# First edge stage of a graph network: target terms from limbs kept in SBUF, two one-hots and two products per tile

## What is computed

```
h = (x @ W).reshape(-1, H, F)
el = (h * attn_l).sum(-1)
er = (h * attn_r).sum(-1)
e = leaky_relu(el[src] + er[dst], 0.2)
emax = segment_max(e, dst)
ee = exp(e - emax[dst])
alpha = ee / segment_sum(ee, dst)[dst]
rst = segment_sum(h[src] * alpha[:, :, None], dst)
```

## Time and profile before

| what | value |
|---|---|
| median of 3 runs | 12361.57 us (12352.24 to 12380.39) |
| profiled execution, its own time | 12351.98 us |
| its span in the trace | 12350.2 us |
| node stage of layer 0 writes its tables | 176 to 205 us |
| first edge stage | 205 to 3578 us |
| last edge stage | 9832 to 12284 us |
| transfers of limbs | 1632 of 3.0 KB |
| gathers of the first edge stage | 1612 |

### The profile page before, as it was taken

One profiled execution on the slowest core, in us unless ns is written; L12 is line 12 of the kernel. 1 busy time (PEld: TensorE's weight loads), 2 busy tenths in 40 slices (PEclk: granted clock), 3 DMA queues, 4 the chain that ended last, 5 costly groups with the idle time before them and its releaser, 6 DMA issues. The chain is left out here.

```text
span 12350.2 us, 151587 instructions
## 1 busy us (share of the span) xinstructions
PE 6147.4 (50%) x29478; PEld 5149.9 (42%) x29478; DVE 6427.4 (52%) x17554; ACT 1847.1 (15%) x3224; POOL 7271.6 (59%) x6460
## 2 busy tenths in 40 slices
PE   1332333333345555555554677777777644444443
PEld 1222222222234444455454566666666533333332
DVE  3444444444456777666666566666666533332234
ACT  0111111111112222211111111111111200000001
POOL 2445444544517888888887455555555466666664
PEclk7555555555555555555555788788777755555555
DMA  3322322223256677777777211111111111111111
GB/s 84 75 76 70 77 75 72 74 75 76 71 102 111 111 108 111 112 108 110 113 108 117 55 39 39 39 39 40 40 38 39 43 44 43 43 43 43 44 43 44
DMA packets 1090391, 862.21 MB, mean 70 GB/s; under 512 B 408696, under 2 KB 925183, under 8 KB 1089702
## 3 DMA queue, kind: packets, MB, share of 16 engines
q0 software_dynamic: 386880, 430.42, 20.5%
q1 hardware_dynamic: 702220, 427.58, 14.0%
q10 hardware_dynamic: 1036, 1.96, 0.1%
HBM read 709.41 MB, written 149.81 MB: 70 GB/s over the span
## 5 line engine op out<-in xcount | busy, mean ns | idle before, releaser
L1274 POOL DMA_INDIRECT sums<-sumrows,index x1612 | 2527.6, 1568 | 710.4 <-issue 311.3
L663 POOL DMA_INDIRECT rows<-table,index x1612 | 1614.1, 1001 | 1890.4 <-DMA index<-in_src_batches 1414.4
L1415 POOL DMA_INDIRECT rows<-table,index x1612 | 1587.7, 985 | 1298.1 <-DVE mid L1472 741.9
L1611 POOL DMA_INDIRECT rows<-table,index x1612 | 1530.6, 949 | 1010.5 <-issue 475.6
L1672 PE MATMUL psS<-hot,rows 128*128 128x128 f32 x3224 | 1024.0, 476 | 1445.0 <-issue 655.4
L1672 PEld LDWEIGHTS psS<-hot,rows 128*128 128x128 f32 x3224 | 793.5, 313 | 1675.4 <-issue 888.9
L801 DVE TENSOR_TENSOR ACC<-ACC,psA 128x128 f32 x1612 | 462.9, 287 | 1682.3 <-remote 836.3
L1242 PE MATMUL psX<-same,hotW 128*128 128x128 f32 x3224 | 811.2, 431 | 987.3 <-DVE hotW L1145 744.7
L1242 PEld LDWEIGHTS psX<-same,hotW 128*128 128x128 f32 x3224 | 702.8, 321 | 1109.1 <-DVE hotW L1145 849.4
L1644 DVE TENSOR_TENSOR ACC<-ACC,psS 128x128 f32 x1612 | 465.8, 289 | 1258.6 <-issue 686.6
L1506 PEld LDWEIGHTS psS<-hot,mid 128*128 128x128 f32 x6448 | 1092.6, 240 | 64.1 <-issue 3.0
(11 more groups left out here) (306 smaller groups left out, 9781.0 us busy)
## 6 DMA issues: line engine op xcount, KB each, us to landing
win<-table SPq DMA_DIRECT2D x1612, 64.5 KB
srow<-src_f SPq DMA_DIRECT2D x403, 256.0 KB
rows<-table,index POOLq DMA_INDIRECT x4836
HN<-rel_f SPq DMA_DIRECT2D x102, 512.0 KB, 4.4
relB<-rel_f SPq DMA_DIRECT2D x102, 512.0 KB, 6.1
er<-limbs SPq DMA_DIRECT2D x1632, 3.0 KB
sums<-sumrows,index POOLq DMA_INDIRECT x1612
ACC<-edge_marks SPq DMA_DIRECT2D x204, 96.0 KB
```

Of the source, the lines that this page charges most:

```text
L663: nc.gpsimd.indirect_dma_start(out=rows[:, r, k, :], out_offset=None, in_=table0[:, :], in_offset=bass.IndirectOffsetOnAxis(ap=index[:, r, ...
L1274: nc.gpsimd.indirect_dma_start(out=sums1[u][:, :], in_=sums[:, s, u, :], in_offset=None, compute_op=ALU.add, out_offset=bass.IndirectOffse ...
L1415: nc.gpsimd.indirect_dma_start(out=rows[:, n % R, u, :], out_offset=None, in_=table2[:, :], in_offset=bass.IndirectOffsetOnAxis(ap=index[: ...
L1611: nc.gpsimd.indirect_dma_start(out=rows[:, n % R, u, :], out_offset=None, in_=table3[:, :], in_offset=bass.IndirectOffsetOnAxis(ap=index[: ...
```

## The change

The limbs of all nodes stay in SBUF as `LIMB`, 128 nodes by 50 blocks (the last of zeros), and are not written to DRAM. A tile's destinations lie in the block of its first destination or the next one. Positions are relative to the start of that block, 0 to 255, so ScalarE makes two one-hots (own block and the next, `far`), and TensorE takes two products which accumulate. The block number is a register on PE, read from `B0F` by `blocks`. SP loads no limbs. Three of the four zero fills are issued behind the loads of batches 3, 4 and 5.

```diff
-        D0 = sb("D0", [1, T], I32)
+        first_rows = sb("first_rows", [2 * 32, T], I32)
+        D0, B0F = first_rows[0:1, :], first_rows[32:33, :]
+        LIMB = sb("LIMB", [P, TN + 1, 3, H], BF16)
...
+        def blocks(eng, tile):
+
+            _, firsts = nc.values_load_multi_w_load_instructions(
+                B0F[0:1, bass.ds(tile, U)], engines=(eng.engine,), min_val=0, max_val=N // P,
...
                             sp.wait_ge(s_limbs, 1)
-                            sp.dma_start(limbs[0:TN * P, :].rearrange("(t p) c -> p t c", p=P), LIMB[:, :, :, :].rearrange("p t l h -> p t (l h)")).then_inc(s_out, 16)
-                            sp.dma_start(limbs[TN * P:NPAD, :], LIMB[:, 0, :, :].rearrange("p l h -> p (l h)")).then_inc(s_out, 16)
-                        sp.wait_ge(s_out, 32 if limbs is None else 64)
+                        sp.wait_ge(s_out, 32)
...
-                        nc.vector.tensor_tensor(rel[:, :, :], edge[:, :, :], first, ALU.subtract).then_inc(s_rel, 1)
+                        link(nc.vector.tensor_scalar(block_i[:, :, :], edge_i[:, :, 0:1], ~(P - 1), None, ALU.bitwise_and))
+                        link(nc.vector.tensor_copy(block_v[:, :, :], block_i[:, :, :]))
+                        nc.vector.tensor_tensor(rel[:, :, :], edge[:, :, :], block_v[:, :, :].to_broadcast([TP, TT, P]), ALU.subtract).then_inc(s_rel, 1)
...
-                        dve.wait_ge(s_in, 16 * 5)
+                        dve.wait_ge(s_in, 16 * 6)
                         nc.vector.tensor_copy(src_v[:, :], src_i[:, :]).then_inc(s_float, 1)
+                        link(nc.vector.tensor_scalar(B0F[:, :], B0F[:, :], 7, None, ALU.logical_shift_right))
...
-            hotT = sb("hotT0", [P, 2, PIECE, P], BF16)
+            hotT = sb("hotT0", [P, 2, 2, PIECE, P], BF16)
...
                         for q in range(pieces):
-                            for k in range(q * PIECE, (q + 1) * PIECE):
-                                if k % U == 0:
-                                    firsts = windows(sp, n * B0 + k)
-                                sp.dma_start(er[:, r, k, :], limbs0[bass.ds(firsts[k % U], P), :]).then_inc(s_erw[r], 16)
-                        for q in range(pieces):
-                            wait_over(sp, s_hotT, (n - 1) * pieces + (q + 1))
+                            wait_over(sp, s_abs, (n - 1) * pieces + (q + 1))
...
+                    for r in range(R):
+                        load(R + r, 1, r)
+                        zeros(r)
+                    with sp.Fori(2, BATCHES // R) as g:
                         for r in range(R):
                             load(R * g + r, g, r)
-                    for k in range(COPIES):
-                        sp.dma_start(sums1[k].rearrange("(t p) c -> p t c", p=P), K[:, CZ:CEND].unsqueeze(1).to_broadcast([P, NPAD // P, W1])).then_inc(s_clear, 16)
+                    zeros(R)
...
-                            nc.scalar.activation(relB[q], relB[q], ACT.Abs, bias=K[:, CN:CN + 1]).then_inc(s_abs, 1)
+                            own, far = (hotT[:, q % 2, b, :, :].rearrange("p t e -> p (t e)") for b in range(2))
+                            nc.scalar.activation(far, relB[q], ACT.Abs, bias=K[:, CF:CF + 1]).then_inc(s_far, 1)
+                            nc.scalar.activation(own, relB[q], ACT.Abs, bias=K[:, CN:CN + 1]).then_inc(s_abs, 1)
+                            act.wait_ge(s_far, n * pieces + (q + 1))
+                            nc.scalar.activation(far, far, ACT.Relu, bias=K[:, C1:C1 + 1], scale=-1.0)
                             act.wait_ge(s_abs, n * pieces + (q + 1))
-                            nc.scalar.activation(own, relB[q], ACT.Relu, bias=K[:, C1:C1 + 1], scale=-1.0).then_inc(s_hotT, 1)
+                            nc.scalar.activation(own, own, ACT.Relu, bias=K[:, C1:C1 + 1], scale=-1.0).then_inc(s_hotT, 1)
...
-                        pe.wait_ge(s_erw[r], 16 * B0 * g + 16 * B0)
...
-                                done = nc.tensor.matmul(psE[:, k * 3 * H:(k + 1) * 3 * H], hotT[:, q % 2, k % PIECE, :], er[:, r, k, :], start=True, stop=True)
+                                if k % U == 0:
+                                    starts = blocks(pe, n * B0 + k)
+                                own = psE[:, k * 3 * H:(k + 1) * 3 * H]
+                                nodes2 = LIMB[:, bass.ds(starts[k % U], 2), :, :]
+                                nc.tensor.matmul(own, hotT[:, q % 2, 0, k % PIECE, :], nodes2[:, 0, :, :].rearrange("p l h -> p (l h)"), start=True, stop=False)
+                                done = nc.tensor.matmul(own, hotT[:, q % 2, 1, k % PIECE, :], nodes2[:, 1, :, :].rearrange("p l h -> p (l h)"), start=False, stop=True)
```

More of the change, by code:

```diff
@@ L51, in constants @@
     k[:, C1] = 1.0
+    k[:, CF] = -(P + np.arange(P))
     k[0:3, CO:CZ] = 1.0
@@ L190, in windows @@
                 D0[0:1, bass.ds(tile, U)], engines=(eng.engine,), min_val=0, max_val=N,
+                skip_runtime_bounds_check_because="a dst is a node number, and padding edges end at N")
+            return firsts
+        def blocks(eng, tile):
+            _, firsts = nc.values_load_multi_w_load_instructions(
+                B0F[0:1, bass.ds(tile, U)], engines=(eng.engine,), min_val=0, max_val=N // P,
                 skip_runtime_bounds_check_because="a dst is a node number, and padding edges end at N")
@@ L280, in _ @@
                             value = TAB[:, :, width - H:width]
-                            link(nc.vector.tensor_copy(LIMB[:, :, 0, :], value))
-                            link(nc.vector.tensor_tensor(rest[:, :, :], value, LIMB[:, :, 0, :], ALU.subtract))
-                            link(nc.vector.tensor_copy(LIMB[:, :, 1, :], rest[:, :, :]))
-                            link(nc.vector.tensor_tensor(rest[:, :, :], rest[:, :, :], LIMB[:, :, 1, :], ALU.subtract))
-                            nc.vector.tensor_copy(LIMB[:, :, 2, :], rest[:, :, :]).then_inc(s_limbs, 1)
+                            nc.vector.memset(limbs[:, TN:TN + 1, :, :], 0.0)
+                            link(nc.vector.tensor_copy(limbs[:, 0:TN, 0, :], value))
+                            link(nc.vector.tensor_tensor(rest[:, :, :], value, limbs[:, 0:TN, 0, :], ALU.subtract))
+                            link(nc.vector.tensor_copy(limbs[:, 0:TN, 1, :], rest[:, :, :]))
+                            link(nc.vector.tensor_tensor(rest[:, :, :], rest[:, :, :], limbs[:, 0:TN, 1, :], ALU.subtract))
+                            nc.vector.tensor_copy(limbs[:, 0:TN, 2, :], rest[:, :, :]).then_inc(s_limbs, 1)
                     @block.scalar
@@ L476, in build @@
                 edge = sb("edge", [TP, TT, P])
+                block_i = sb("block_i", [TP, TT, 1], I32)
+                block_v = sb("block_v", [TP, TT, 1])
                 ends_i = sb("ends_i", [BATCHES, 4, B0], I32)
@@ L500, in _ @@
                         sp.dma_start(src_i[:, :], flat(a["src_rows"])).then_inc(s_in, 16)
-                        sp.dma_start(D0[:, :], a["dst_first"]).then_inc(s_in, 16)
+                        for row in (D0, B0F):
+                            sp.dma_start(row[:, :], a["dst_first"]).then_inc(s_in, 16)
                         sp.wait_ge(s_rel, 1)
@@ L565, in _ @@
                         link(nc.vector.tensor_tensor(REL[:, :], REL[:, :], first_v, ALU.subtract))
-            node_stage(0, W0, table0, load0, 3, prepare0, limbs=limbs0)
+            node_stage(0, W0, table0, load0, 3, prepare0, limbs=LIMB)
         with ExitStack() as st:
@@ L614, in build @@
             s_rows = gathered0
-            s_index, s_erw, s_marks, s_rowm = (sem(n, R) for n in ("s_index_e0", "s_erw_e0", "s_marks_e0", "s_rowm_e0"))
+            s_index, s_marks, s_rowm = (sem(n, R) for n in ("s_index_e0", "s_marks_e0", "s_rowm_e0"))
             s_rel = sem("s_rel_e0", pieces)
@@ L643, in _, with zeros @@
                     load(2, 0, 2)
[L644 removed]
+                    def zeros(k):
+                        sp.dma_start(sums1[k].rearrange("(t p) c -> p t c", p=P), K[:, CZ:CF].unsqueeze(1).to_broadcast([P, NPAD // P, W1])).then_inc(s_clear, 16)
+                    for r in range(R):
+                        load(R + r, 1, r)
+                        zeros(r)
+                    with sp.Fori(2, BATCHES // R) as g:
                         for r in range(R):
                             load(R * g + r, g, r)
[L647 to L648 removed]
+                    zeros(R)
                     for r in range(R):
```

12 lines of the change are left out of this document (3 added, 9 removed).

## The result

The changed kernel takes 12,793.7 us (median of 4, 12,782.3 to 12,821.6) against 12,364.2 for the kernel before on the same chip: ratio 1.035, interval 1.0329 to 1.0371, so 430 us **slower**, outside the range of the prediction. The profiled execution took 12,821.6 us, 470 more than that of before.

The account below looks back on a forecast made before the run. VectorE's chain in the first edge stage, slowed while gathers are issued, was taken as the bound (65.7 us per batch). Terms −10 − 9 + 3 − 20 + 2 + 0 = −34 took 12,352 to 12,318 us; range 12,070 to 12,520.

Parts of the forecast that it names:

- (1): Products and one-hots at the first edge stage's batch boundary: longer chain, +3.8 us per ordinary batch, mean 3.4.
- (2): SP's 32 limb loads gone from each first-edge-stage batch: VectorE gets 3.4 us back, cancelling (1) over 49 batches.
- Step (6): One more column in the constants and PE's longer loop body: nothing to be seen, 0 us.
- rival E: PE's loop restart in the first edge stage becomes visible: 8 rounds × 3.34 = +27 us, 12,345 us; chance 0.03.
- Step (3): Start of the first edge stage: gathers 1 and 2 follow without their pauses, −10 us.
- (4): Node stage: without the limb write the table write ends the stage, −9 us; two small preparation operations, +3 us.
- (5): End of the first edge stage: three of four zero fills move earlier, −20 us, and +2 for the moved ones.
- B: Slower, at the batch boundary: no queue relief or PE's piece at its high end, +167 us, 12,485 us; chance 0.30.
- C: More relief per batch: PE's piece at 2.0 us and 4.4 us given back in full, −123 us, 12,195; chance 0.21.
- D: Limb loads cause the slow queues in the first edge stage: batch falls to 46 us, −946 us, 11,372; chance 0.10.

Follow-up runs that it names:

- late_targets_3: The kernel before with ScalarE writing each one-hot piece five times, PE's loop untouched, third run, on a slow chip: 1.0299 times before, +352 us.
- experiment 7: The changed kernel with its products in nested loops on PE to shorten PE's big loop, on a fast chip: 1.0989 times the kernel before.
- experiment 5: The kernel before with 38 tiny products per batch on PE where no gather is issued: 0.9997 on a fast chip, 1.0001 on a slow one.
- experiment 6: The kernel before with ScalarE writing each one-hot piece five times: 1.0178 and 1.0168 on fast chips, 1.0299 on a slow one.
- experiment 9: The changed kernel with each batch's gathers held until the boundary's products are done, on a slow chip: 1.0273 times the kernel before, +328 us.
- experiment 3: The kernel before with limbs loaded for the first three batches only: 0.9985 (−14 us) on a fast chip, 0.993 (−79 us) on a slow one.

## Why the prediction was wrong

**The step that failed** is that (1) and (2) cancel, "0 × 49 batches". Measured: +448 us over 47 batches of the first edge stage. It failed in two places, the price of the longer chain and the price of the longer program, and a little in the relief. Of the other terms only the start was far off.

**Step (1), the chain of products, in size: right.** Where nothing else is slow, the target comes 12.4 to 12.6 us behind the index load (changed kernel on A3; 12.5 with the gathers delayed on B1; forecast 12.5), and the batch costs 3.9 us more (forecast 3.8). *What failed is the step from there to the time*, "+3.8 us" per batch, one for one. On the chip of the result the gathers start 2.4 us after the index load, VectorE is slow for the 40 us that they take, and more of the chain's end now falls inside this time: the target comes at about 16 and not at 12.5. Priced without PE's fetches, later one-hots that cost 3.5 us a batch on A3 (170/49) cost 7.3 on B2 (late_targets_3), twice as much. In the result the 25 ordinary intervals are 71.9 − 65.7 = 6.2 longer.

**Step (6) and rival E, the longer program: mechanism in part right, price wrong in kind.** PE's loop is now fetched, 83 packets against 5. The Trainium skill ("Advanced Engine Details and Errata", section "ISA Cache") has 128 KB on TensorE in lines of 16 KB; the trace agrees with the lines, 1.36 MB in 83 packets. The size at which fetching begins isn't shown: experiment 7's loop, 1725 instructions by the listing, an estimated 108 KB by that page, was fetched as well. I priced the fetch as a stall at the loop's restart, 0 in the sum and +27 in rival E. Where only the loop is longer, the restart costs no more than before (experiment 5). Instead the products, which moved under the gathers, crawl there when PE's code comes in between. The price is the long batches: 11 pairs of 158.1 instead of 2 × 71.9, 11 × 14.3 = 157 us. With 47 × 6.2 = 291 for the rest this makes the 448; that it does is arithmetic, since both parts are read from the same intervals. The evidence for the parts is elsewhere: a loss without PE's fetches and without long batches in experiment 6, the fetches without a loss in experiment 5, and no long batch with the gathers delayed in experiment 9.

**Step (2), the relief: half.** 3.4 forecast, 1.9 on B1, nothing on A1. With it the two would not have cancelled even at face value: +3.8 − 1.9 is about +2 a batch. By the page of the Trainium skill that the prediction cites ("SBUF — State Buffer", section "SBUF: two separate sides") the relief would have been 0; the trace agrees with that on A1 and not on B1, and what it shows there is in the issue of instructions, which that rule doesn't cover.

**Step (3), the start: wrong.** Batch 0 was forecast 10 us shorter. The node stage ended 17 us earlier, and by the third target 8 us had been lost, so the start cost 25 us where −10 was forecast. Beside the first gathers, PE's third product piece took from 211 to 237 us, one product per 1.4 us, the fourth started at 261, and VectorE made its first target only at 332.43 instead of 270.33, behind the gathers of three batches.

**Steps (4) and (5): right in kind.** The limb write gave −13 (forecast −9), and the preparation's +3 is not seen: it is −4 in the one profile and 0 in the other. The end gave −23 (forecast −20 and +2).

**The rivals.** B had the sign and the place, and a price of 3.4 a batch where 448/47 = 9.5 was paid: it too added the chain at its face value. C and D are refuted by experiment 3. E had the fetch, and put it where it costs nothing. None joined the two effects: a chain that ends later under the gathers, and PE slow there when its code is fetched.

**What stays open.** Why VectorE in a long batch waits until the last gather is issued (30.66 us, "remote"), and not only until PE's products are done, isn't settled; no packet of code starts in that wait. The change and late_targets were not run together on one slow chip, so that the ordinary part of the loss is the chain's rests on two chips and on 6.2 us against 7.3. What makes VectorE slow under gathers on some chips and not on others is not known.

## What to carry to other kernels

A delay ahead of a stretch in which an engine is slow can cost more than itself (here some 4 us became 6 to 7), so price the chain by where it ends, not by its length. Count an engine's loop body before adding instructions to it: a loop that has to be fetched was harmless here on a chip without slow queues, and where the added instructions ran outside the gathers; it was costly where they ran beside gathers on a slow chip. Compare kernels only on one chip, and ask whether a result would hold on the other kind.

## What the runs showed of the hardware

- The same kernel takes 10.0, 12.15 or 12.37 ms depending on the chip, at the same granted clock of 0.51 in the first edge stage; the difference lies in the three stages where GpSimd issues gathers of table rows back to back. Its idle time before them is 780, 514 and 570 us in the first, third and last edge stage on A1, and 1890, 1298 and 1011 on the chip of the prediction.
- On the slow kind, VectorE and SP are slow while GpSimd issues gathers back to back (VectorE busy for 1.76 of 21 us), and PE is too once its loop is fetched: its tiny products one per 1.4 to 3.5 us, its register instructions up to 1.4 us instead of 0.046. It is a connection, and the mechanism isn't shown; in the run with the tiny products the register instructions of the sums stay at 32 to 36 ns.
- Fetching PE's code cost nothing by itself on B1: 86 packets of 16 KB, ratio 1.0001 (0.999 to 1.0012).
- PE's loop of the kernel before needs 5 packets in the stage, those of the first pass; the one with 38 products more in each of its six batches needs 85.
